# Taking the turned row maxima out of PSUM on ScalarE instead of VectorE in two dense attentions

## The reference

```
attn = jnp.einsum('bhnd,bhmd->bhnm', q, k) * scale
attn = jax.nn.softmax(attn, axis=-1)
attn_out = jnp.einsum('bhnm,bhmd->bhnd', attn, v)
```

```
qk = jnp.einsum('bhqd,bhkd->bhqk', q, k)
qk = qk / jnp.float32(np.sqrt(s))
p = jax.nn.softmax(qk, axis=-1)
mask = jnp.triu(jnp.ones((s, s), dtype=p.dtype), k=0)
p = p * mask
z = jnp.einsum('bhqk,bhkd->bhqd', p, v)
```

## Time and profile before

| | |
|---|---|
| median of 3 runs | 1895.95 us (1893.87 to 1903.23) |
| the profiled execution | 1902.14 us, its span 1900.3 us |
| first attention's exponentials | 114.05 us to 446 us |
| second attention's exponentials | 1038.88 us to 1387 us |
| TensorE, VectorE, ScalarE, GpSimd busy | 85%, 74%, 59%, 32% of the span |

### The profile page before, as it was taken

How to read it: one execution, slowest core, us unless ns; L and a number is a source line. 1 busy time by engine, 2 the same in 40 slices (tenths; PEclk the granted TensorE clock), 3 DMA queues, 4 the chain that set the end, 5 groups by cost and what they waited for, 6 DMA issues and landing times. The chain is left out here.

```text
span 1900.3 us, 29630 instructions
## 1 busy us (share of the span) xinstructions
PE 1610.1 (85%) x11092; PEld 878.9 (46%) x11120; DVE 1406.9 (74%) x2091; ACT 1130.6 (59%) x2178; POOL 604.5 (32%) x494
## 2 busy tenths in 40 slices
PE   6489999997598786988866999999865999989897
PEld 4112222223366653666540333333234777767775
DVE  3799999982777447764446999999635887878697
ACT  2348888884477534775351777777733545545453
POOL 1830000002476325763022222222211453435354
PEclk8679999998699986999875999999976998989899
DMA  2230011001111001110004211110011000000000
GB/s 70 68 116 18 18 29 23 1 1 48 28 29 29 21 20 30 34 29 16 1 15 128 66 21 21 21 21 4 7 25 51 1 0 0 0 0 0 0 0 22
DMA packets 56776, 49.14 MB, mean 26 GB/s; under 512 B 37800, under 2 KB 41256, under 8 KB 56016
## 3 DMA queue, kind: packets, MB, share of 16 engines
q1 hardware_dynamic: 56016, 45.29, 9.2%
q10 hardware_dynamic: 576, 2.16, 0.3%
q0 software_dynamic: 64, 0.07, 0.0%
HBM read 24.34 MB, written 14.68 MB: 21 GB/s over the span
## 5 line engine op out<-in xcount | busy, mean ns | idle before, releaser
L821 ACT ACTIVATE att_probs<-psum 128x512 f32<-128x512 f32 x1024 | 536.3, 605 | 200.6 <-PE psum L749 199.9
L832 DVE TENSOR_REDUCE att_neg_max<-psum 128x1 f32<-128x1024 f32 x512 | 600.8, 1219 | 45.9 <-PE psum L720 40.1
L720 PE MATMUL psum<-att_k_op,att_q_op 48*128 48x512 bf16 x1024 | 350.8, 409 | 56.5 <-DMA att_k_op<-qk_parts 34.9
L749 PE MATMUL psum<-att_q_op,att_k_op 50*128 50x512 bf16 x1024 | 314.1, 387 | 19.6 <-ACT att_probs L821 19.6
L1841 ACT ACTIVATE moe_hidden<-psum,moe_b 128x512 f32<-128x512 f32 x256 | 169.1, 691 | 137.1 <-PE psum L76 116.8
L767 PE MATMUL psum<-att_probs,att_v 128*32 128x512 f32 (+2 forms) x1664 | 203.8, 559 | 2.9 <-ACT att_sums L813 2.8
L749 PEld LDWEIGHTS psum<-att_q_op,att_k_op 50*128 50x128 bf16 x1024 | 78.0, 94 | 251.9 <-ACT att_probs L821 188.7
L64 DVE CAST moe_hidden_high<-moe_hidden 128x512 fp32r<-128x512 f32 x256 | 149.1, 600 | 41.6 <-ACT moe_hidden L1841 41.4
L1870 POOL TENSOR_TENSOR moe_hidden_low<-moe_hidden,moe_hidden_high 128x512 fp32r<-128x512 f32 x64 | 107.0, 1671 | 203.3 <-DVE moe_hidden_high L64 203.3
L908 POOL TENSOR_TENSOR att_diag<-att_probs,att_triangle 128x512 f32<-128x512 f32 x64 | 81.8, 1278 | 272.2 <-PE psum L770 176.8
L720 PEld LDWEIGHTS psum<-att_k_op,att_q_op 48*128 48x128 bf16 x1024 | 72.4, 95 | 180.7 <-DVE att_neg_max L832 120.1
(11 more groups left out here) (235 smaller groups left out, 2922.8 us busy)
## 6 DMA issues: line engine op xcount, KB each, us to landing
wl_v_shift<-wl_v SPq DMA_DIRECT2D x62, 128.0 KB, 2.2
att_q_op<-qk_parts SPq DMA_DIRECT2D x32, 192.0 KB, 3.4
att_k_op<-qk_parts SPq DMA_DIRECT2D x32, 192.0 KB, 4.4
qk_parts<-att_hi SPq DMA_DIRECT2D x12, 256.0 KB
qk_parts<-att_hi SPq DMA_DIRECT2D x12, 192.0 KB
qk_parts<-att_mid SPq DMA_DIRECT2D x8, 256.0 KB
moe_w<-in_moe_w SPq DMA_DIRECT2D x2, 1024.0 KB, 6.1
qk_parts<-att_mid SPq DMA_DIRECT2D x8, 192.0 KB
```

The costliest lines, as they stand in the source:

```text
L720: mm = pe.matmul(buf[:, half * CHUNK:(half + 1) * CHUNK], q_op[it % RING][at_rows(p, MAX_ROW), j, t * P:(t + 1) * P], k_op[it % RING][at_r ...
L749: pe.matmul(st_bank[e % 3], k_op[it % RING][at_rows(p, MAX_ROW + 2), j, t * P:(t + 1) * P], q_op[it % RING][at_rows(p, MAX_ROW + 2), j, ha ...
L821: act.activation(probs[:, g % PB, h, :], st_bank[e % 3], ACT.Exp, scale=scale).then_inc(exp_done, 1)
L832: dve.tensor_reduce(neg[:, t, p, j:j + 1], ring[e % 2], AX.X, ALU.max, negate=True).then_inc(ring_free, 1)
```

## The change

ScalarE takes the turned maxima. Where the entry of the ring was made at the end of step 5, ScalarE copies it in step 6, between the second and the third exponential. The first entry of each attention it copies ahead of its loop. Such an entry is now released by a semaphore of its own, `rows_taken`, and no longer counts in `ring_free`. So every count of `ring_free` is lowered by the `rows` entries before it (`rows_upto`), and `claim` and the DMA issue in `rows` wait for the one or the other.

```
+        rows_upto = list(accumulate([0] + [int(kind == "rows") for kind, _ in order]))
...
             def rows(n):
...
-                sp.wait_ge(ring_free, number["rows", n] + 1)
+                sp.wait_ge(rows_taken, n + 1)
...
             def claim(e):
-                if number[e] >= 2:
-                    pe.wait_ge(ring_free, number[e] - 1)
+                gone = number[e] - 1
+                if gone > 0:
+                    if order[gone - 1][0] == "rows":
+                        pe.wait_ge(rows_taken, rows_upto[gone])
+                    else:
+                        pe.wait_ge(ring_free, gone - rows_upto[gone])
                 return ring[number[e] % 2]
...
+            def take_rows(n):
+                e, it, half = number["rows", n], n // 2, n % 2
+                act.wait_ge(ring_ready, e + 1)
+                if it:
+                    act.wait_ge(m_rows[half], 32 * it)
+                act.activation(neg_rows[:, half * CHUNK:(half + 1) * CHUNK], ring[e % 2][0:2 * GROUP, 0:CHUNK], ACT.Copy)\
+                   .then_inc(rows_taken, 1)
+
+            take_rows(0)
             for g in range(LAST):
                 for i, h in enumerate(heads_of(g)):
                     e = GROUP * g + i
+                    if i == 2 and g:
+                        for kind, n in entries(g - 1):
+                            if kind == "rows":
+                                take_rows(n)
                     act.wait_ge(st_ready, e + 1)
...
-            def rows(n):
-                e, it, half = number["rows", n], n // 2, n % 2
-                dve.wait_ge(ring_ready, e + 1)
-                if it:
-                    dve.wait_ge(m_rows[half], 32 * it)
-                dve.tensor_copy(neg_rows[:, half * CHUNK:(half + 1) * CHUNK], ring[e % 2][0:2 * GROUP, 0:CHUNK])\
-                   .then_inc(ring_free, 1)
```

More of the change, by code:

```diff
@@ L11 @@
 from contextlib import ExitStack, contextmanager
+from itertools import accumulate
 import numpy as np
@@ L597, in attention @@
             "triangle_loaded")))
-    (z_stored,) = sems(nc, f"{tag}_z_stored")
+    z_stored, rows_taken = sems(nc, f"{tag}_z_stored", f"{tag}_max_rows_taken")
     m_rows = sems(nc, *(f"{tag}_max_rows_loaded{half}" for half in range(2)))
@@ L677, in store_z @@
                 b, g = it // GROUPS, it % GROUPS
-                sp.wait_ge(ring_free, number["turn", 2 * it + 1] + 1)
+                last = number["turn", 2 * it + 1] + 1
+                sp.wait_ge(ring_free, last - rows_upto[last])
                 for j in range(GROUP):
@@ L832, in maximum @@
                 dve.tensor_reduce(neg[:, t, p, j:j + 1], ring[e % 2], AX.X, ALU.max, negate=True).then_inc(ring_free, 1)
+                taken = e + 1 - rows_upto[e + 1]
                 if (m + 1) % (2 * SEQ_TILES) == 0:
@@ L835, in maximum @@
                     at = slice(n % 2 * 4, n % 2 * 4 + 4)
-                    dve.wait_ge(ring_free, e + 1)
+                    dve.wait_ge(ring_free, taken)
                     dve.tensor_copy(neg_parts[:, at, :, 0, :], neg[:, at, :, :]).then_inc(hi_done, 1)
@@ L853, in turn @@
                 if n + 1 == HALVES:
-                    dve.wait_ge(ring_free, e)
+                    dve.wait_ge(ring_free, e - rows_upto[e])
                 tile = ring[e % 2][:, 0:CHUNK].rearrange("p (t h c) -> p t h c", t=4, c=32)
@@ L865, in _ @@
                     maximum(arg)
-                elif kind == "rows":
-                    rows(arg)
-                else:
+                if kind == "turn":
                     turn(arg)
```

## The result

The changed kernel takes 1932.63 us (median of 4 runs, 1926.86 to 1934.69) beside 1897.01 us for the kernel before (4 runs, 1893.87 to 1903.23). The ratio is 1.0178, with a 95% interval of 1.0152 to 1.0204. By that ratio it is about 34 us more, by the two medians 35.6, where 25.3 were forecast, and 1932.6 lies above the range of 1909 to 1930. The profiled execution took 1931.58 us, its span 1929.8.

What follows compares the result with a forecast made beforehand. No busy engine but the loop over TensorE's written order bounds an ordinary step. 21 x 0.88 + 7 x 0.97 = 25.3 us on the median 1895.95 makes 1921.3 us, 1.3% slower, own range 1916 to 1927, wider 1909 to 1930.

Steps and rivals of the forecast that it cites:

- The removal, costed at nothing: VectorE's copy, 0.67 us each, lies in a hole VectorE has anyway for the ring's refill; removing it wins nothing.
- that rival (VectorE is the bound): VectorE is the bound and the copy's slot is won: 28 x 0.78 = 21.8 us faster, 1874 us; chance 0.04.
- The copy's length: ScalarE's copy takes 0.57 us, from a near measured copy; bounds 0.48 and 0.67 us, 0.52 by the skill's overheads.
- Its place and who waits: In step 6 the copy ends 0.96 us later, TensorE's maxima B wait; net 0.88 or 0.97 us a half.
- Nothing for the first and the last entry: Each attention's first rows entry, and a moved table load of 1.28 us, cost nothing; the last under 0.05 us.
- The clock: TensorE's idle time lowers its clock after each copy: some 2 us each, 55 us in all; chance 0.05 with table loads.
- the sum: 14 halves in each attention lose time: 21 x 0.88 + 7 x 0.97 = 25.3 us, added to the median.
- The noise: The range 1916 to 1927 takes in some 3 us that the three runs of the kernel before differ by.

Runs made afterwards that it cites:

- experiment 4: Changed kernel with ScalarE's copy ahead of the first exponential of step 6 in place of the third: 1895.37 us, ratio 0.9981.
- Experiment 3: Changed kernel with overwritten matmuls filling both TensorE waits of step 6, three ahead of the maxima B, two ahead of the maxima A: 1928.49 us, ratio 1.0157.
- experiment 5: Changed kernel with ScalarE's copy ahead of the second exponential of step 6: 1902.0 us, ratio 1.0024.
- experiment 6: Changed kernel with ScalarE's copy ahead of the fourth exponential of step 6: 1959.56 us, ratio 1.032.
- experiment 7: Changed kernel with TensorE in step 6 doing score 2, score 3, the values, then both halves of the maxima B: 1923.88 us (one run).
- experiment 8: Changed kernel with the turned rows in a score bank, not the ring, copied by ScalarE ahead of step 6's first exponential: 1883.48 us, again 1883.4 us.
- experiment 9: Changed kernel with the turned rows in a score bank, but copied by VectorE behind its second reduction of step 5: 1897.19 us, ratio 0.9997.
- experiment 2: Changed kernel with three overwritten matmuls at the end of step 6, behind the values, where TensorE doesn't wait: 1955.11 us (one run).

## Why the prediction fell short

**The removal, costed at nothing: right.** The reduction behind the old copy's place starts 0.04 us after its fill, with 0.70 us idle in front, in the changed kernel and in experiment 4. The 22 us of that rival (VectorE is the bound) did not come, although VectorE's busy share suggested them.

**The copy's length: right.** 0.57 us taken, 569 ns measured. The estimate of 0.52 us from the Trainium skill, "Perfetto Trace Analysis", section "Optimizing Scalar/DVE Operations", was 0.05 us too low. The measurement decides.

**Its place and who waits: right, to 0.01 us.** Step 6 was forecast at 3.86 us and measured at 3.86, step 7 at 2.39 and 2.39. The halves without a fall grew by 0.88 us in the first attention (21.66 for 20.78), and by 0.89 and 0.97 in the second, as forecast. Experiment 3 isolates this term: 24.9 us, for 25.3. Experiments 4 to 6 show how it goes with the place.

**Nothing for the first and the last entry: right.** The table load did move behind the copy in the second attention, and its end, near 1050.2 us, leaves ScalarE idle 3.60 us ahead of the first exponential:

```profile
1048.31 0.59 ACT L827 ACTIVATE att_neg_rows<-psum 8x512 bf16<-8x512 f32 x1 [36.01 <-PE psum L738]
1048.91 1.28 ACT L841 ACT_TABLE_LOAD   x1
1053.79 2.31 ACT L841 ACTIVATE att_probs<-psum 128x512 f32<-128x512 f32 x4 [3.60 <-PE psum L756]
```

**The clock: this step failed.** The prediction put a lower clock among the rivals, at 0.05 together with the table loads, left it out of the sum, and waved it off: the 0.40 us of waiting there was at clock 1.00, "and 0.96 us more is no long stretch." Nine of 28 such steps lost the full clock, at about 1.2 us each, 10.6 us in all. With the 25.3 us of the sum that makes 35.9, for the 35.6 measured. The rival was mis-sized too, at 2 us each and in every half. What it lacked was the middle case, that some of them fall, and this belonged in the range. That the late hand-off brings the falls is shown: the kernels in which TensorE doesn't wait for a late copy of ScalarE's have none (before, experiments 4, 5, 7 to 9), and with a wait 0.48 us longer there are 16. In the first attention filling that wait ended them and the same work elsewhere didn't. In the second the falls went only when a wait was filled that the kernel before has too, so there it is not shown that the wait for ScalarE alone makes them. The Trainium skill, "TensorE: Matmul & The Clock Gate", section "A second HAM failure mode: psum-queue depth-cycling", tells of small idle spots between groups of matmuls, frequent enough that the clock swings between its two levels. The trace agrees in kind, with waits of 0.39 and 0.73 us in one step.

What stays open is which of the steps fall: why every second half in the first attention, and why one filled wait was enough there and not in the second. Neither the length of the waits nor their sum decides it alone: in the changed kernel and in experiment 2 steps with the same waits go both ways, and experiment 7 waits longer in all, further apart, without a fall. When in time a step comes, and how closely its waits follow each other, are the rivals that no run here tells apart.

**The noise: misread, and not what failed.** The range allows some 3 us for what the three runs before differ by. They differ by 1903.23 - 1893.87 = 9.4 us.

## What to carry to other kernels

Before work is moved off an engine that looks full, look at what ends its next wait. If it is a refill of a ring that the moved entry still occupies, nothing is won, and the engine that takes it over sets the release by its own order. A late release costs its delay times the number of steps whose loop it lies on, and here TensorE's longer wait brought a lower clock in some of the steps on top, so the range has to reach to that. What paid was to give the entry a buffer whose drainer meets it in its natural order.

## What the runs showed of the hardware beyond that

In the changed kernel a wait of TensorE well under a microsecond (0.73 us), added to one of 0.39 us in the same step, went with a halved clock for some three microseconds in nine of 28 such steps, at an average busy share of TensorE above 0.9 (269.78 of 290 us):

```profile
150.00:440.00 290.00, 269.78 (x1779) 66.99 (x1774) 255.97 (x260) 230.77 (x444) 2.40 (x6) 0.96 0.06 15
```

The number behind the window's length is TensorE's busy time. In experiments 3 and 7 the clock is 1.00 in the same stretch, and so it is in the window of the kernel before. In experiment 7 TensorE is busy no longer than here, 269.33 us of the same 290. The busy share of a stage doesn't tell whether the clock falls in it. A mean clock of 0.96 over a stage is a sign worth following down to single steps.
